# A cross-attention kernel: the output projection in four quarters, the row maxima spread by ScalarE, and one tile product issued behind the product of sums

## The reference

```python
x = (hidden_states - mu) * rsqrt(var + 1e-5) * ln_gamma + ln_beta
Q = split_heads(x @ Wq.T)            # 32 heads of 16
K = V = split_heads(context)         # 32 x 1500 x 512
scores = where(mask, einsum('bhsd,bhtd->bhst', Q, K) * 16 ** -0.5, -inf)
attn = einsum('bhst,bhtd->bhsd', softmax(scores), V)
out = hidden_states + merge_heads(attn) @ Wout.T
```

## Time and profile before

| | |
|---|---|
| runs (three) | 1614.45, 1623.83, 1624.25 us; median 1623.83 |
| profiled execution, its own time | 1620.93 us |
| its span, first to last instruction | 1619.2 us |
| mean granted TensorE clock in it | 0.961 of full speed |
| busy: PE, VectorE, ScalarE, GpSimd | 89%, 67%, 44%, 69% of the span |
| first exponential starts, last one starts | 142.16 us, 1599.19 us |

### The profile page before, as it was taken

How to read it: one execution, slowest core, us unless ns; L and a number is a source line. 1 busy time by engine, 2 the same in 40 slices (tenths; PEclk the granted TensorE clock), 3 DMA queues, 4 the chain that set the end, 5 groups by cost and what they waited for, 6 DMA issues and landing times.

```text
span 1619.2 us, 65921 instructions
## 1 busy us (share of the span) xinstructions
PE 1437.3 (89%) x30080; PEld 1022.8 (63%) x30080; DVE 1078.9 (67%) x3340; ACT 720.4 (44%) x495; POOL 1122.4 (69%) x403
## 2 busy tenths in 40 slices
PE   4888989999999999998999999899998999999986
PEld 3335666666666666666666666666666666666664
DVE  6334767777777677767677677677777777776730
ACT  1123444444445444444445454444544444444443
POOL 1002767787878777878678687777777787887776
PEclk7788989999999999999899999989999999999998
DMA  9201444444444454444334444434444444443320
GB/s 284 58 0 59 156 150 146 149 162 150 149 146 146 153 165 149 158 152 143 122 131 164 157 158 141 154 133 142 154 142 166 147 162 149 146 161 132 129 82 7
DMA packets 39160, 224.89 MB, mean 139 GB/s; under 512 B 4546, under 2 KB 4578, under 8 KB 26882
## 3 DMA queue, kind: packets, MB, share of 16 engines
q1 hardware_dynamic: 38882, 220.68, 40.8%
HBM read 216.90 MB, written 3.77 MB: 136 GB/s over the span
## 4 chain that ended last, share of the span: by engine, by line
PE 67%; ACT 17%; DVE 8%; issue 6%; DMA 1%; SPq 1%; POOL 0%; ACTq 0%; DVEq 0%; POOLq 0%
PE ps L261 20%; ACT probs L353 16%; PE ps L224 14%; PE ps L276 13%; PE ps L290 7%; PE ps L253 6%; DVE masked L311 6%; PE ps L631 4%; PE ps L239 4%; DVE den_inv L342 1%; DMA v<-in_x 1%; ACT sums L593 1%; DVE tile_max L311 1%; SPq L415 0%; ACTq L352 0%
## 5 line engine op out<-in xcount | busy, mean ns | idle before, releaser
L311 DVE CUSTOM_DVE_ANT_0 masked<-ps,mask_tile 112x500 bf16<-112x500 f32 x1536 | 974.3, 672 | 418.4 <-PE ps L224 407.9
L353 ACT ACTIVATE probs<-ps,mask_bias 125x1792 f32<-125x1792 f32 x384 | 674.0, 1755 | 763.8 <-PE ps L261 759.1
L389 POOL TENSOR_TENSOR sums<-probs 125x1792 f32<-125x1792 f32 x128 | 512.3, 4003 | 452.5 <-ACT probs L353 452.5
L224 PE MATMUL ps<-kT,qdb 32*112 32x500 bf16 x1536 | 517.9, 416 | 49.4 <-DVE tile_max L311 31.3
L261 PE MATMUL ps<-qd,kT 32*125 32x112 f32 x12288 | 518.7, 278 | 7.3 <-issue 7.3
L393 POOL TENSOR_TENSOR sums<-sums,probs 125x1792 f32<-125x1792 f32 x128 | 510.7, 3990 | 19.8 <-ACT probs L353 11.5
L261 PEld LDWEIGHTS ps<-qd,kT 32*125 32x125 f32 x12288 | 498.6, 187 | 9.4 <-issue 8.6
L276 PE MATMUL ps<-probs,v 125*32 125x112 f32 x12288 | 380.4, 264 | 0.8 <-issue 0.5
L276 PEld LDWEIGHTS ps<-probs,v 125*32 125x32 f32 x12288 | 301.3, 111 | 76.5 <-issue 60.3
L224 PEld LDWEIGHTS ps<-kT,qdb 32*112 32x112 bf16 x1536 | 160.2, 124 | 197.2 <-DVE tile_max L311 137.6
L253 PE MATMUL ps<-max_rows,ones_row 4*125 4x448 bf16 x1536 | 169.7, 399 | 87.9 <-ACT probs L353 87.5
(11 more groups left out here) (45 smaller groups left out, 231.0 us busy)
## 6 DMA issues: line engine op xcount, KB each, us to landing
kT<-in_kt SPq DMA_DIRECT2D x96, 1000.0 KB, 6.2
v<-in_ctx SPq DMA_DIRECT2D x96, 1000.0 KB
mask_tile<-mask_add SPq DMA_DIRECT2D x32, 328.1 KB, 15.0
x_res<-in_x SPq DMA_DIRECT2D x16, 224.0 KB, 16.1
out<-result SPq DMA_DIRECT2D x16, 224.0 KB, 3.6
probs<-in_x SPq DMA_DIRECT2D x14, 224.0 KB, 9.3
v<-in_wq_t SPq DMA_DIRECT2D x1, 1024.0 KB, 6.1
woutT<-in_wout_t SPq DMA_DIRECT2D x1, 1024.0 KB, 21.0
```

Source lines behind the costliest of these rows:

```text
L224: nc.tensor.matmul(bank[0:PAIR_Q, 0:KEYS], qdb[rows, b % 2, g, :], keys, start=True, stop=True).then_inc(ring_filled, 1)
L311: nc.vector.tensor_tensor_reduce(out=masked[0:PAIR_Q, t % 2, :], in0=bank[0:PAIR_Q, 0:KEYS], in1=mask_tile[0:PAIR_Q, b % 2, KEYS * c:KEYS ...
L353: nc.scalar.activation(probs[0:LANES, k % PROBS], ps[0:LANES, 0:TILES_R, 0:BANK_Q], ACT.Exp, bias=mask_bias[0:LANES, n:n + 1], scale=SCALE ...
L389: nc.gpsimd.tensor_tensor(total, probs[0:LANES, slot % PROBS], probs[0:LANES, (slot + 1) % PROBS], ALU.add).then_inc(summed, 1)
```

## The change

There are four edits.

1. **Projection in quarters.** `project_out` computes 128 of 512 columns at a time (four products of 128 columns instead of 512). The quarters are ring units of their own, placed behind t3 in slot 9 of the even batch and in slots 0, 1 and 3 of the odd one that follows (`OUT_AT`). The last pair's four quarters stand at the end of the program. `add_residual` takes each quarter.
2. **Rows by ScalarE.** `spread_rows` moves from VectorE to ScalarE, where it is four instructions of 128x112 instead of one of 128x448. It stands behind the exponential of slot 10, and for batch 0 ahead of the first exponential. A semaphore of its own, `rows_taken`, tells PE; `wait_taken` picks the right one for each ring unit.
3. **Third tile behind the product of sums.** In sum slots t2 is issued after `add_denominators`. In other slots nothing changes.
4. **Store.** The store of a pair's result moves from the end of an even batch to the odd batch after it, ahead of the load of the residual rows; there are as many DMAs of the same size.

```diff
+OUT_PARTS = 4
+OUT_COLS = HIDDEN // OUT_PARTS
+OUT_AT = [(0, 9), (1, 0), (1, 1), (1, 3)]
...
-    if k == OUT_SLOT and b % 2 == 0 and b > 0:
-        units += [("out", b // 2 - 1)]
+    if (b % 2, k) in OUT_AT and b > 1:
+        units += [("out", b // 2 - 1, OUT_AT.index((b % 2, k)))]
...
+        def wait_taken(eng, unit):
+            if unit[0] == "rows":
+                eng.wait_ge(rows_taken, unit[1] + 1)
+            else:
+                eng.wait_ge(ring_taken, TAKEN_AT[unit] + 1)
...
-            wait_over(pe, ring_taken, RING_AT[unit] - 1)
+            if RING_AT[unit] >= 2:
+                wait_taken(pe, RING[RING_AT[unit] - 2])
...
-                mm = nc.tensor.matmul(bank[0:PAIR_Q, 0:HIDDEN], attnT[:, g, :], woutT[:, g, :],
+                mm = nc.tensor.matmul(bank[0:PAIR_Q, 0:OUT_COLS], attnT[:, g, :],
+                                      woutT[:, g, OUT_COLS * part:OUT_COLS * (part + 1)],
...
+        def spread_rows(act, b):
+
+            act.wait_ge(ring_filled, filled_past(("rows", b)))
+            if b >= 2:
+                act.wait_ge(scored, SLOTS * (b - 1))
+            for g in range(BLOCKS):
+                ins = nc.scalar.activation(max_rows[:, b % 2, g, :], bank_of(("rows", b))[:, 0:PAIR_Q], ACT.Copy,
+                                           scale=own_block[:, g:g + 1])
+            ins.then_inc(rows_taken, 1)
...
+                    if k == ROWS_SLOT and b < end:
+                        spread_rows(act, b + 1)
...
-                    if tiles:
+                    sums_ready = k >= 5 and k % 3 == 2 or k == 2 and b > 0
+                    if tiles and not sums_ready:
                         score_tile(pe, tiles[2])
-                    if k >= 5 and k % 3 == 2:
-                        add_denominators(pe, b, k // 3 - 1)
-                    elif k == 2 and b > 0:
-                        add_denominators(pe, b - 1, SUMS - 1)
+                    if sums_ready:
+                        add_denominators(pe, *((b, k // 3 - 1) if k > 2 else (b - 1, SUMS - 1)))
+                        if tiles:
+                            score_tile(pe, tiles[2])
```

More of the change, by code:

```diff
@@ L61 @@
 RING += [unit for b in range(BATCH) for k in range(SLOTS) for unit in slot_tiles(b, k) + slot_others(b, k)]
-RING += [("out", BATCH // 2 - 1)]
+RING += [("out", BATCH // 2 - 1, part) for part in range(OUT_PARTS)]
 RING_AT = {unit: n for n, unit in enumerate(RING)}
+TAKEN_AT = {unit: n for n, unit in enumerate(unit for unit in RING if unit[0] != "rows")}
 def build(nc, x, kt, ctx, mask_lanes, mask_rows, wq_t, wout_t, gamma, beta, out):
@@ L247, in begin_scores @@
             if k == 0:
-                pe.wait_ge(ring_taken, filled_past(("rows", b)))
+                wait_taken(pe, ("rows", b))
                 pe.wait_ge(qd_ready, b + 1)
@@ L300, in take_unit @@
                 take_tile(dve, unit[1], unit[2], bank_of(unit))
-            elif unit[0] == "rows":
-                spread_rows(dve, unit[1], bank_of(unit))
             else:
-                add_residual(dve, unit[1], bank_of(unit))
+                add_residual(dve, unit[1], unit[2], bank_of(unit))
         def take_tile(dve, b, t, bank):
@@ L316, in take_max @@
         def take_max(dve, b):
-            dve.wait_ge(ring_taken, filled_past(("tile", b, MAX_TILES - 1)))
+            wait_taken(dve, ("tile", b, MAX_TILES - 1))
             if b > 0:
-                dve.wait_ge(ring_taken, filled_past(("rows", b - 1)))
+                dve.wait_ge(ring_filled, filled_past(("rows", b - 1)))
             nc.vector.tensor_reduce(neg_max[0:PAIR_Q, :, 0:BLOCKS],
@@ L322, in take_max, with add_residual @@
                                     AX_X, ALU.max, negate=True).then_inc(neg_ready, 1)
-        def spread_rows(dve, b, bank):
-            if b >= 2:
-                dve.wait_ge(scored, SLOTS * (b - 1))
-            nc.vector.tensor_tensor(max_rows[:, b % 2], bank[:, 0:PAIR_Q].unsqueeze(1).broadcast_to([128, BLOCKS, PAIR_Q]),
-                                    own_block[:, :].unsqueeze(2).broadcast_to([128, BLOCKS, PAIR_Q]), ALU.mult
-                                    ).then_inc(ring_taken, 1)
-        def add_residual(dve, d, bank):
+        def add_residual(dve, d, part, bank):
+            cols = slice(OUT_COLS * part, OUT_COLS * (part + 1))
             dve.wait_ge(res_landed, 16 * d + 16)
             wait_over(dve, result_stored, 16 * d)
-            nc.vector.tensor_tensor(result[0:PAIR_Q, :], bank[0:PAIR_Q, 0:HIDDEN], x_res[0:PAIR_Q, :], ALU.add
+            nc.vector.tensor_tensor(result[0:PAIR_Q, cols], bank[0:PAIR_Q, 0:OUT_COLS], x_res[0:PAIR_Q, cols], ALU.add
                                     ).then_inc(ring_taken, 1)
@@ L402, in divide_heads @@
             if b % 2 == 0 and b > 0:
-                pool.wait_ge(ring_filled, filled_past(("out", b // 2 - 1)))
+                pool.wait_ge(ring_filled, filled_past(("out", b // 2 - 1, OUT_PARTS - 1)))
             pool.wait_ge(heads_added, b + 1)
@@ L454, in _ @@
                     if b + 2 < BATCH:
-                        sp.wait_ge(ring_taken, filled_past(("tile", b, MAX_TILES - 1)))
+                        wait_taken(sp, ("tile", b, MAX_TILES - 1))
                         load_mask(sp, b + 2)
                 if b % 2 == 1:
+                    if b > 1:
+                        store_result(sp, b // 2 - 1)
                     load_residual(sp, b // 2)
@@ L464, in _ @@
                     load_v(sp, b + 1, 1)
-                if b % 2 == 0 and b > 0:
-                    store_result(sp, b // 2 - 1)
             store_result(sp, BATCH // 2 - 1)
@@ L561, in _ @@
                 take_unit(dve, unit)
-            take_unit(dve, ("rows", 0))
             for b in range(BATCH):
@@ L573, in _ @@
                     for unit in slot_others(b, k):
-                        take_unit(dve, unit)
+                        if unit[0] == "out":
+                            take_unit(dve, unit)
             for g in range(BLOCKS):
                 invert_denominators(dve, end, g)
-            take_unit(dve, ("out", BATCH // 2 - 1))
+            for part in range(OUT_PARTS):
+                take_unit(dve, ("out", BATCH // 2 - 1, part))
         @block.scalar
@@ L599, in _ @@
                             std(later_unit)
+            act.wait_ge(consts, CONSTS)
+            spread_rows(act, 0)
             act.wait_ge(mask_added, 2)
@@ L671, in _ @@
             add_denominators(pe, end, SUMS - 1)
-            project_out(pe, ("out", BATCH // 2 - 1))
+            for part in range(OUT_PARTS):
+                project_out(pe, ("out", BATCH // 2 - 1, part))
 FILL_PLAN = [(kind, u, c) for u in range(UNITS) for kind in ("x", "q") for c in range(BLOCKS)]
```

10 lines of the change are left out of this document (6 added, 4 removed).

## The result

The changed kernel takes 1624.4 us (median of 20 runs, 1619.16 to 1632.87), the one before 1612.7 us beside it (20 runs, 1597.98 to 1629.65), which is 12 us less. The ratio, which leaves out runs of over 1.5% above the fastest of their kernel (five of the kernel before, none of the changed one), is **1.0104, 95% interval 1.0078 to 1.0129**: 17 us slower. The forecast was 1646 on a profiled execution of 1620.9, that is +25, with 0.66 for slower by over 1%. Slower it is; whether by over 1% is not settled, as the interval reaches down to 0.78%.

A forecast was written before the change was run, and what follows sets the result against it. PE (89% busy) was taken to bound sum slots by its window's end, ordinary slots having 0.53 us idle. Third tile +45, quarters -20, rows +0.4, last pair -0.3 gave +25 on 1620.93: 1646 us, range 1612 to 1667.

The forecast's parts named there:

- Third tile: Sum slots: t2 standing alone behind the sums makes `begin_scores` 0.37 us later, 122 times, +45 us (ends +21 and +65).
- Whatever makes PE's window longer lengthens the slot in full: Sum slots, 3.75 us: PE and ScalarE finish together, no idle time before `begin_scores`, so added PE time lengthens the slot.
- the last step of the sum: End of a sum slot's window: t3 and t0 take 0.27 us to `begin_scores`, giving 943.97 instead of 943.60.
- that wait of t1 for t3: Slot behind a sum slot: t1 waits until VectorE has taken t3, at unchanged distance, so VectorE gives none of 0.37 back.
- The first rival: Sum slots: PE waits unseen 0.3 us or more before `begin_scores`, so t2 costs nothing; 1601 us, chance 0.08.
- Quarters: Slots 9, 0, 1, 3: quarters of 0.97 us add 2.18 instead of 3.50 a pair; -1.32, 15 pairs, -20 us.
- Rows by ScalarE: Slot 10: four copies take 1.07 us, done 0.12 before t1 of slot 11; cost 0 (upper end +9), +0.4 once at the start.
- Drain in full: Sum slots: both steps around the lone t2 wait for the full records before them; +65 us, 1666 us, chance 0.08.
- The sum: Whole kernel: +45 - 20 + 0.4 - 0.3 = +25 on the profiled 1620.93, giving 1646 us.

The follow-up runs named there:

- f2: Kernel before plus one 288-column product in a 32-row tile between sums and values of sum slots (times only); ratio 1.0201, sum slot 4.15 us.
- f3: Kernel before plus one 288-column product in a 32-column tile, same kind as its neighbours, between sums and values (times only); ratio 1.0070, sum slot 3.88 us.
- e1: Kernel before with only the third tile moved behind the product of sums; ratio 1.0172, sum slot 4.13 us.
- e2: Changed kernel with the third tile put back in its old place, the other edits kept; ratio 0.9923 to the kernel before, sum slot 3.75 us.
- f1: Kernel before with the exponential of sum slots split into three instructions, nothing added on PE; ratio 1.0013, sum slot still 3.75 us.
- g4: Changed kernel with t1 issued behind all score products in slots 0, 3, 6 and 9; ratio 1.0046 to the kernel before, sum slot 3.58 us.
- e3: Kernel before with only the rows on ScalarE and the moved store, projection whole, third tile in its old place; ratio 0.9999.

## Why the prediction was right, and what it missed

- **Third tile: right on its price.** +0.37 a sum slot forecast, 0.38 measured, 122 times. f2 and f3 show the two steps between kinds of tile as the larger part of the price (0.27 of it). e1 shows the edit to be the whole of the slowdown, e2 the rest of the change to be a gain (0.9923).
- **"Whatever makes PE's window longer lengthens the slot in full": wrong as the reason.** `begin_scores` has 0.3 of room (f1), and the last step of the sum, 0.27 from t3 and t0 to `begin_scores`, holds in the changed kernel for the last of its four products alone (0.28; the first starts 0.05 after t3), while in the earlier trace rows the first waited for the exponential. The slot is set by t3 and VectorE's 1.20 behind it. The prediction named that wait of t1 for t3, but only to say that it gives nothing back. The sum came out because the moved tile delays t3 by the same 0.38; that the wrong end of the slot gave the right price is luck. Where t1 doesn't decide (g4), the window's end does, at 0.34. The first rival had the room in sight (it asked for 0.37 between t0 and `begin_scores`) but drew from it that the move would be free; f1 shows the room, and e1 that it doesn't help.
- **Quarters: right in mechanism, a little less.** -1.32 a pair forecast, -1.07 measured. The mis-sized term is the quarter, 1.06 instead of 0.97. The prediction took one step of 0.09 out of the whole block and shared out the remainder. But the block has such a step at both ends: its second pass starts 0.52 after the first and t0 0.53 after the last, the others 0.43 apart. A quarter pays both: passes 0.11 apart, but 0.20 behind the first one and 0.21 from the last to t0. Slots 9, 0, 1 and 3 are 0.56, 0.56, 0.50 and 0.83 longer for it instead of 0.48 three times and 0.74. The weight loads hid behind the short passes, as forecast.
- **Rows by ScalarE: right.** 0 forecast, and nothing found but the eight late exponentials, 1.4 us (e3). The four copies take 0.354 each and 1.09 together (1.07 forecast), and t1 doesn't wait. By ScalarE: Activation LUTs in the Trainium skill, What ACT_TABLE_LOAD costs, each would take 0.37 and the four 1.21 (an estimate); the trace is 0.1 below it.
- **Drain in full** (TensorEngine Tiling (Array Packing) in the Trainium skill, Key Properties): the trace doesn't bear it out as a full drain. Sums to the lone tile is 0.90 with a record of 0.96, the tile to the values 0.35 with one of 0.42. That it costs something to change modes is right (0.27 there and back, f2 and f3).
- **The sum: the step that was missed** is the one not written, that stalls and clock stay as they were. Slots say +30, the forecast said +25. By the ratio 17 were measured, so 13 of the 30 came back, and by the medians, 12 apart, 18 did, since longer sum slots leave almost no stalls and no half clock. In the two profiled executions, 1.5 apart, it was 19 us of 28 batches, more than in a typical run, as the one before lies 8 above its median. The forecast of 1646 is 22 above the measured median: 8 of that are the base, 13 the change itself (+25 against +12 by the medians). That the result lies within the stated range owes something to its width of 55 us.

## What to carry to other kernels

A slot whose engines finish together has more than one chain through it; before pricing an edit by "no idle time here", follow also the tile that another engine must hand back, and delay the suspected end by itself (a split instruction does it) to see whether the slot moves. A small product placed among others of its own kind of tile cost a third of what it cost between two of another kind (0.13 and 0.40 us). And where a loop uses up PE's instructions at a high rate, time given by an edit may be taken back by stalls for instructions and by the clock behind them: compare undisturbed slots and the rest apart, since the totals mix both.
